# Attention: the causal mask added by VectorE in the score bank instead of by TensorE

## The chip, the cores and the metric

The kernel runs on one core of one Trainium2 chip. The time is device time in microseconds of one execution; the text compares medians of several executions. Of the core's engines four compute: TensorE (PE in the profile; its weight loads are PEld), VectorE (DVE), ScalarE (ACT) and GpSimd (POOL). SyncE (SP) issues the DMAs.

## The reference

Four layers with residual sums: causal attention, a mixture of experts, a state-space layer, the same mixture again. The change lies in the attention:

```python
x = x + attn(layernorm(x))                       # x: 2 x 1024 x 128
qk = x @ W_qk;  q, k = split(qk)                 # 16 heads of 64; k serves as the values too
scores = einsum('bhid,bhjd->bhij', q * 64**-0.5, k)
scores = where(triu(ones(n, n), k=1), -finfo.max, scores)
attn = softmax(scores, axis=-1)
out = einsum('bhij,bhjd->bhid', attn, k)  ...  @ W_out
```

## The kernel before

Attention works through 16 units (`UNITS`), each one batch entry and one pair of heads; head l of a pair lies on partitions 64 l to 64 l + 63. The scores are made transposed: keys on the partitions, queries along the bank. Key tile j (128 keys) meets only query tiles from j on, and `SLOTS` packs these stretches into 9 slots of 512 columns for each head of the pair. A slot is a pair of banks. A tile with query tile = key tile is a diagonal one; there are 8 in a unit, in slots 0 (one), 1, 2 (two each), 7 (one) and 8 (two). In slots 1 and 8 the second tile stands alone, a stretch of 128 columns.

To subtract each row's maximum ahead of the exponential, the scores are made once more the other way round one unit earlier, in 10 maxima fills (`MAX_FILLS`), which VectorE reduces (`maxima`: L498 with the mask `after_query` where the fill holds a diagonal tile, L494 without). The joined maxima are turned by TensorE (`turn_max`, L600), spread by VectorE (`max_rows`, L512), and added into the scores as a last matmul of each stretch (L625). Before that matmul a stretch has three products of high and low parts (L616, L618, L620) and, on a diagonal tile, four matmuls in bfloat16 of 128 columns that add the mask (L623: `mask2` times the unit matrix `eye2`, for two halves h and two heads l).

All of these fills share a ring of three pairs of banks (`ring`, `ring_uses`). A unit uses it in the order T (turned keys of the next unit), slot 0, Q (query projection of the next unit), slot 1, maxima fill 0, slot 2, fill 1, slot 3, fill 2, slot 4, fills 3 and 4, slot 5, fill 5, slot 6, fills 6, 7 and 8, slot 7, fill 9, slot 8, K (key projection of the unit after next). `pair_free` makes TensorE wait until the reader of the fill three places before has finished: ScalarE's exponential for a slot (`exponentials`, L453), VectorE's maxima for a fill, ScalarE's and VectorE's copies for K and Q.

The order on each engine is written out in five rounds (`ROUNDS`). At the head of round r TensorE runs a burst of output matmuls of the previous unit (`outputs`, L643), in rounds 1 and 3 also the denominators (`denominators`, L656). The outputs of round 0 and of round 1 need their bank back from VectorE's rescaling (`scale_out`, L521, semaphore `out_used`). GpSimd adds up the exponentials (`add_up`, L378), ScalarE inverts the denominators (L444, L446) and copies keys and queries (L423, L424, L429, L435), VectorE makes their low parts (L485, L314). The loops that the change touches:

```python
ROUNDS = [[("S", 0)], [("S", 1), ("M", 0), ("S", 2), ("M", 1)], [("S", 3), ("M", 2), ("S", 4), ("M", 3), ("M", 4)],
          [("S", 5), ("M", 5), ("S", 6), ("M", 6), ("M", 7)], [("M", 8), ("S", 7), ("M", 9), ("S", 8)]]
```

"S" is a slot of this unit, "M" a maxima fill of the next. The last unit has no "M".

## Time and profile before

| | |
|---|---|
| median of 3 runs | 796.08 us (795.87 to 797.96) |
| profiled execution | 797.62 us |
| its span, first to last instruction | 795.8 us, granted TensorE clock 0.983 on the mean |
| attention's units | from about 42 to 496 us of the span |
| score matmuls of the mask (L623) | 512, all between 43.8 and 488.2 us |

The profile comes from one execution. Its rows name engine, line, operation and tiles by the program's names, with the tile written before the arrow. Busy time of TensorE is that of modelled ends, so that overlapping matmuls count for more than the queue spends on them; the starts of successive rows are the better measure. In a timeline a row merges several alike instructions (x2, x4); its length then runs from the start of the first to the end of the last. Idle time ahead of a row stands in brackets with what ended it.

### The profile page before, as it was taken

What the parts mean: (1) busy time and instruction counts of PE and PEld (TensorE: products, weight loads), DVE (VectorE), ACT (ScalarE), POOL (GpSimd) and SP (SyncE); (2) the same over time, 40 slices, a digit from 0 to 9 for tenths busy, and PEclk for the clock granted to TensorE, in tenths of its full rate; (3) what the DMA queues carried; (4) which work ended last, traced back from release to release, by engine and by line L of the source; (5) the groups of instructions that cost most, each with busy time, mean ns of one, the idle gap of its engine ahead of it and who ended that gap; (6) DMA issues with size and microseconds to landing.
All of it is one profiled execution on the core that took longest, in us unless ns stands there. A gap on an engine that the chain in (4) does not pass through costs nothing. (4 is left out here: it accounts for less than half of the span.)

```text
span 795.8 us, 14382 instructions
## 1 busy us (share of the span) xinstructions
PE 738.3 (93%) x5520; PEld 499.9 (63%) x5520; DVE 455.8 (57%) x1216; ACT 386.8 (49%) x476; POOL 429.4 (54%) x311
## 2 busy tenths in 40 slices
PE   2789999999999999999999998999989999689998
PEld 1456556555655655655655554887878875468887
DVE  5765665665565675565566540257565547665542
ACT  2355546545555555554654544235753543465421
POOL 3346865765675685685676568015455331345443
PEclk9699999999999999999999999999999999799999
DMA  2000000000000000000000000733233000033232
GB/s 66 7 2 1 2 8 1 7 2 1 8 2 1 8 1 1 8 2 1 1 2 1 28 1 1 174 80 100 77 93 92 17 1 0 2 109 105 92 99 80
DMA packets 29752, 25.56 MB, mean 32 GB/s; under 512 B 10162, under 2 KB 21236, under 8 KB 29684
## 3 DMA queue, kind: packets, MB, share of 16 engines
q1 hardware_dynamic: 29684, 24.64, 10.6%
q8 instruction: 44, 0.72, 0.4%
q14 instruction: 24, 0.20, 0.1%
HBM read 23.32 MB, written 1.31 MB: 31 GB/s over the span
## 5 line engine op out<-in xcount | busy, mean ns | idle before, releaser
L378 POOL TENSOR_TENSOR all_x<-all_x,at_probs 128x1024 f32<-128x1024 f32 (+3 forms) x128 | 221.9, 1733 | 35.7 <-ACT at_probs L453 21.0
L453 ACT ACTIVATE at_probs<-at_ring 128x1024 f32<-128x1024 f32 x144 | 147.2, 1023 | 114.1 <-PE at_ring L625 107.3
L498 DVE CUSTOM_DVE_ANT_0 at_ring<-at_ring,at_after_query 128x128 f32<-128x128 f32 (+3 forms) x256 | 119.5, 520 | 74.4 <-PE at_ring L590 74.4
L643 PE MATMUL at_out<-at_probs,at_k_nat 128*64 128x512 f32 (+3 forms) x768 | 140.3, 494 | 1.1 <-DVE a_attn_t L521 0.9
L1091 POOL TENSOR_TENSOR m_prod<-m_gate,m_wb 128x512 f32<-128x512 f32 x64 | 83.0, 1304 | 97.7 <-ACT m_gate L946 93.6
L378 POOL TENSOR_TENSOR all_x<-at_probs 128x768 f32<-128x768 f32 (+1 forms) x32 | 67.1, 2095 | 126.7 <-ACT at_probs L453 126.6
L643 PEld LDWEIGHTS at_out<-at_probs,at_k_nat 128*64 128x64 f32 x768 | 49.2, 136 | 69.9 <-issue 66.0
L494 DVE TENSOR_REDUCE at_half_max<-at_ring 128x2 f32<-128x1024 f32 x64 | 75.4, 1221 | 12.2 <-PE at_ring L590 12.2
L1000 DVE TENSOR_TENSOR m_hid<-m_prod,m_u 128x512 f32<-128x512 f32 x64 | 43.4, 685 | 66.4 <-POOL m_prod L1091 66.2
L616 PE MATMUL at_ring<-at_qh,at_kh 64*128 64x512 f32 (+3 forms) x384 | 73.6, 380 | 6.2 <-DVE at_m_rows L512 2.6
L866 PEld LDWEIGHTS m_acc<-rest_wd,m_hid 128*128 128x128 f32 x576 | 74.7, 191 | 5.9
L625 PE MATMUL at_ring<-at_m_rows,at_ones_r 64*128 64x512 f32 (+3 forms) x384 | 76.0, 392 | 0.0
L866 PE MATMUL m_acc<-rest_wd,m_hid 128*128 128x128 f32 x576 | 75.2, 275 | 0.0
L946 ACT ACTIVATE m_gate<-m_g 128x512 f32<-128x512 f32 x72 | 42.6, 598 | 66.3 <-PE m_g L858 65.0
L590 PE MATMUL at_ring<-at_kh,at_qh 64*128 64x512 f32 (+3 forms) x384 | 65.5, 390 | 8.5 <-DVE at_half_max L498 2.4
L616 PEld LDWEIGHTS at_ring<-at_qh,at_kh 64*128 64x128 f32 x384 | 36.5, 187 | 52.8 <-issue 37.2
L618 PE MATMUL at_ring<-at_ql,at_kh 64*128 64x512 f32 (+3 forms) x384 | 67.0, 345 | 0.0
L620 PE MATMUL at_ring<-at_qh,at_kl 64*128 64x512 f32 (+3 forms) x384 | 66.9, 344 | 0.0
L590 PEld LDWEIGHTS at_ring<-at_kh,at_qh 64*128 64x128 f32 x384 | 36.4, 190 | 29.3 <-issue 26.0
L485 DVE TENSOR_TENSOR at_ql<-at_ring,at_qh 128x1024 fp32r<-128x1024 f32 x16 | 19.6, 1225 | 55.5 <-ACT at_qh L429 55.5
L444 ACT ACTIVATE at_inv<-at_misc 128x512 f32<-128x512 f32 x32 | 19.1, 598 | 65.3 <-PE at_misc L656 65.3
L620 PEld LDWEIGHTS at_ring<-at_qh,at_kl 64*128 64x128 f32 x384 | 36.4, 186 | 4.3
(234 smaller groups left out, 1284.1 us busy)
## 6 DMA issues: line engine op xcount, KB each, us to landing
m_wb<-m_wt_far SPq DMA_DIRECT2D x128, 128.0 KB, 3.0
all_x<-in_L_attn_a_x SPq DMA_DIRECT2D x8, 256.0 KB, 3.8
at_w_raw<-in_L_attn_a_W_qk SPq DMA_DIRECT2D x8, 128.0 KB, 2.5
out<-all_x SPq DMA_DIRECT2D x4, 256.0 KB, 3.0
a_room<-in_L_attn_a_W_out SPq DMA_DIRECT2D x1, 512.0 KB, 3.9
m_raw_wg<-in_L_ffn_experts_wg SPq DMA_DIRECT2D x1, 512.0 KB, 4.6
m_raw_wu<-in_L_ffn_experts_wu SPq DMA_DIRECT2D x1, 512.0 KB, 4.2
rest_wd<-in_L_ffn_experts_wd SPq DMA_DIRECT2D x1, 512.0 KB, 4.2
```

Source lines behind the costliest of these rows:

```text
L378: return pool.tensor_tensor(sums[:, :, a * P:b * P], left, right, ALU.add)
L453: act.activation(probs[:, :, slot * BANK:(slot + 1) * BANK], pair("S", unit, slot)[:, :, :], ACT.Exp, scale=BETA).then_inc(exp_done, 1)
L494: last = dve.reduce_max(half_max[:, :, i, out], pair("M", unit, m)[:, :, at:at + w], AX.X)
L498: last = dve.tensor_tensor_reduce(out=sums_ps, in0=sums_ps, in1=after_query[:, BANK - w:BANK], scale=1.0, scalar=MASKED, op0=ALU.add, op1= ...
L590: last = pe.matmul(out[:, l, at:at + (b - a) * P], qh[u][rows(l), i * P:(i + 1) * P], kh[u][rows(l), a * P:b * P], start=True, stop=True)
L616: pe.matmul(to[l], kh[u][rows(l), keys], qh[u][rows(l), q], start=True, stop=False)
L618: pe.matmul(to[l], kh[u][rows(l), keys], ql[u][rows(l), q], start=False, stop=False)
L620: pe.matmul(to[l], kl[u][rows(l), keys], qh[u][rows(l), q], start=False, stop=False)
L625: last = pe.matmul(to[l], ones_r[rows(l), :], m_rows[u][rows(l), q], start=False, stop=True)
L643: last = pe.matmul(out_ps[rows(l), o:o + (b - a) * P], k_nat[g % 3][:, j, rows(l)], probs[:, l, at:at + (b - a) * P], start=(j == 0), stop ...
L866: last = pe.matmul(acc[:, t * P:(t + 1) * P], hid[g % BUFS][:, t * P:(t + 1) * P], f.wd[:, st, :], start=(st == 0 and t == 0), stop=(st == ...
L1091: pool.tensor_tensor(prod[g % BUFS][:, :], gate[g % BUFS][:, :], wb[q % SPREAD][:, :], ALU.mult)\
```

## The change

The bfloat16 tiles `eye2` and `mask2` and the four mask matmuls of a diagonal tile are gone from TensorE. GpSimd makes one 128 x 128 tile `late_key` instead. VectorE gets `mask_scores`: one instruction for a slot with diagonal tiles adds `late_key` to the slot's one or two diagonal tiles of both heads, in the bank. It waits for the slot's scores and signals `masked`, for which ScalarE's exponential of these slots now waits in place of `scores_ready`. On VectorE the add of slot 0 stands ahead of the rescaling in round 0, and the others at the slot's place in the round, in the order of `ROUNDS`.

```diff
--- before.py
+++ after.py
@@ -210,6 +210,7 @@
 NBURST = len(BURSTS)
 ROUNDS = [[("S", 0)], [("S", 1), ("M", 0), ("S", 2), ("M", 1)], [("S", 3), ("M", 2), ("S", 4), ("M", 3), ("M", 4)],
           [("S", 5), ("M", 5), ("S", 6), ("M", 6), ("M", 7)], [("M", 8), ("S", 7), ("M", 9), ("S", 8)]]
+DIAGONAL = [slot for slot in range(NSLOT) if any(a == j for j, a, _ in SLOTS[slot])]
 FIRST_OF_HALF = {0: 0, 1: 1}
 BURST_OF = [max(r for r, b in enumerate(BURSTS) if any(s == slot for s, _ in b)) for slot in range(NSLOT)]
 
@@ -257,7 +258,7 @@
         neg_pick = s.sb("neg_pick", [P, QT])
         ones_r = s.sb("ones_r", [P, P], F32R)
         ones = s.sb("ones", [P, DH])
-        eye2, mask2 = s.sb("eye2", [P, 2, P], BF16), s.sb("mask2", [P, 2, P], BF16)
+        late_key = s.sb("late_key", [P, P])
         after_query = s.sb("after_query", [P, BANK])
 
         ring = [s.stack.enter_context(nc.psum_tensor(f"at_ring{i}", [P, 2, BANK], FP32)) for i in range(3)]
@@ -268,6 +269,7 @@
         proj_ready, hi_done, kt_done = s.sem("proj_ready"), s.sem("hi_done"), s.sem("kt_done")
         k_low, q_low = s.sem("k_low"), s.sem("q_low")
         knat_ps_ready, knat_done = s.sem("knat_ps_ready"), s.sem("knat_done")
+        masked = s.sem("masked")
         max_ready, max_taken, row_max_done = s.sem("max_ready"), s.sem("max_taken"), s.sem("row_max_done")
         rows_ps_ready, rows_done = s.sem("rows_ps_ready"), s.sem("rows_done")
         scores_ready, exp_done, av_done, summed = s.sem("scores_ready"), s.sem("exp_done"), s.sem("av_done"), s.sem("summed_up")
@@ -327,19 +329,16 @@
 
         def set_up(pool):
             split_w(pool, 0)
-            pool.memset(eye2[:, :, :], 0.0).then_inc(consts, 1)
-            pool.memset(mask2[:, :, :], 0.0).then_inc(consts, 1)
+            pool.memset(late_key[:, :], 0.0).then_inc(consts, 1)
             pool.memset(neg_pick[:, :], 0.0).then_inc(consts, 1)
             pool.memset(after_query[:, :], 0.0).then_inc(consts, 1)
-            pool.wait_ge(consts, 4)
+            pool.wait_ge(consts, 3)
             pool.affine_select(out=after_query[:, BANK - P:BANK], in_=after_query[:, BANK - P:BANK], compare_op=ALU.is_ge,
                                fill=MASKED, base=0, pattern=[[-1, P]], channel_multiplier=1).then_inc(consts, 1)
+            pool.affine_select(out=late_key[:, :], in_=late_key[:, :], compare_op=ALU.is_ge, fill=MASKED,
+                               base=0, pattern=[[1, P]], channel_multiplier=-1).then_inc(consts, 1)
             pool.wait_ge(consts, 5)
             for l in range(2):
-                pool.affine_select(out=eye2[rows(l), :, :], in_=eye2[rows(l), :, :], compare_op=ALU.not_equal, fill=1.0,
...
-                pool.affine_select(out=mask2[rows(l), :, :], in_=mask2[rows(l), :, :], compare_op=ALU.is_ge, fill=MASKED,
...
                 pool.affine_select(out=neg_pick[rows(l), :], in_=neg_pick[rows(l), :], compare_op=ALU.not_equal, fill=-1.0,
                                    base=0, pattern=[[-1, QT]], channel_multiplier=1).then_inc(consts, 1)
 
@@ -446,7 +445,10 @@
                     act.activation(inv[half][:, :], inv[half][:, :], ACT.Exp, scale=-1.0).then_inc(inv_done, 1)
 
                 def exponentials(unit, slot):
-                    act.wait_ge(scores_ready, 2 * (NSLOT * unit + slot) + 2)
+                    if slot in DIAGONAL:
+                        act.wait_ge(masked, len(DIAGONAL) * unit + DIAGONAL.index(slot) + 1)
+                    else:
+                        act.wait_ge(scores_ready, 2 * (NSLOT * unit + slot) + 2)
                     if unit:
                         act.wait_ge(av_done, 2 * (NBURST * (unit - 1) + BURST_OF[slot]) + 2)
                         act.wait_ge(summed, NSUM * (unit - 1) + SUMMED_AT[slot] + 1)
@@ -506,6 +508,15 @@
                     wait(dve, rows_ps_ready, 2 * unit)
                     dve.reduce_max(row_max[:, :, 0:QT], half_max[:, :, :, :], AX.X).then_inc(row_max_done, 1)
 
+                def mask_scores(unit, slot):
+
+                    dve.wait_ge(scores_ready, 2 * (NSLOT * unit + slot) + 2)
+                    at = [(at_slot(slot, seg) - slot * BANK) // P for seg, (j, a, _) in enumerate(SLOTS[slot]) if a == j]
+                    tiles = pair("S", unit, slot)[:, :, :].rearrange("p l (s c) -> p l s c", c=P)
+                    own = tiles[:, :, 0:at[-1] + 1:max(at[-1], 1), :]
+                    dve.tensor_tensor(own, own, late_key[:, :].unsqueeze(1).unsqueeze(1).to_broadcast([P, 2, len(at), P]),
+                                      ALU.add).then_inc(masked, 1)
+
                 def max_rows(unit):
 
                     dve.wait_ge(rows_ps_ready, 2 * unit + 2)
@@ -535,11 +546,14 @@
                         if r == 0:
                             if unit == 0:
                                 max_rows(0)
+                            mask_scores(unit, 0)
                             if unit:
                                 scale_out(unit - 1, 0)
                             if more:
                                 queries_low(unit + 1)
                         for what, m in row:
+                            if what == "S" and m in DIAGONAL and r:
+                                mask_scores(unit, m)
                             if what == "M" and more:
                                 maxima(unit + 1, m)
                         if r == NBURST - 1:
@@ -618,9 +632,6 @@
                             pe.matmul(to[l], kh[u][rows(l), keys], ql[u][rows(l), q], start=False, stop=False)
                         for l in range(2):
                             pe.matmul(to[l], kl[u][rows(l), keys], qh[u][rows(l), q], start=False, stop=False)
-                        for h in range(2 if a == j else 0):
-                            for l in range(2):
-                                pe.matmul(to[l][:, 0:P], mask2[rows(l), h, :], eye2[rows(l), h, :], start=False, stop=False)
                         for l in range(2):
                             last = pe.matmul(to[l], ones_r[rows(l), :], m_rows[u][rows(l), q], start=False, stop=True)
                             if seg + 1 == len(SLOTS[slot]):
...
```

(The waits for `consts` of VectorE and TensorE ahead of the first maxima go from 11 to 7.)

TensorE, round 1, slot 1 of a unit, before: the three products and the mask of its first stretch (384 columns), the row maximum, and the second stretch of 128 columns.

```order
L620 MATMUL at_ring<-at_qh,at_kl 128x384 x2
L623 MATMUL at_ring<-at_eye,at_mask 128x128 x4
L625 MATMUL at_ring<-at_m_rows,at_ones_r 128x384 x2
L616 MATMUL at_ring<-at_qh,at_kh 128x128 x2
L618 MATMUL at_ring<-at_ql,at_kh 128x128 x2
L620 MATMUL at_ring<-at_qh,at_kl 128x128 x2
L623 MATMUL at_ring<-at_eye,at_mask 128x128 x4
L625 MATMUL at_ring<-at_m_rows,at_ones_r 128x128 x2
```

The same place after the change, up to the first maxima fill (L604 was L590, L636 was L625):

```order
L634 MATMUL at_ring<-at_qh,at_kl 128x384 x2
L636 MATMUL at_ring<-at_m_rows,at_ones_r 128x384 x2
L630 MATMUL at_ring<-at_qh,at_kh 128x128 x2
L632 MATMUL at_ring<-at_ql,at_kh 128x128 x2
L634 MATMUL at_ring<-at_qh,at_kl 128x128 x2
L636 MATMUL at_ring<-at_m_rows,at_ones_r 128x128 x2
L604 MATMUL at_ring<-at_kh,at_qh 128x128 [waits at_exp_done,at_hi_done]
```

Only the mask matmuls have left; the waits of TensorE are the same. VectorE, from the end of round 4 over round 0 into round 1 of the next unit, before:

```order
L507 TENSOR_REDUCE at_row_max<-at_half_max 128x2x8 [waits at_rows_ps_ready,at_max_taken]
L521 TENSOR_TENSOR a_attn_t<-at_out,at_inv 128x512 [waits at_av_done,at_inv_done]
L512 TENSOR_TENSOR at_m_rows<-at_misc,at_neg_pick 128x1024 [waits at_rows_ps_ready]
L314 TENSOR_TENSOR at_kl<-a_room,at_kh 128x1024 [waits at_hi_done]
L521 TENSOR_TENSOR a_attn_t<-at_out,at_inv 128x512 [waits at_av_done,at_inv_done]
L485 TENSOR_TENSOR at_ql<-at_ring,at_qh 128x1024 [waits at_hi_done]
L498 ISA at_ring,at_half_max<-at_ring,at_after_query 128x128 [waits at_max_ready]
```

The same stretch after the change (L509 was L507, L532 was L521, L523 was L512, L316 was L314, L487 was L485, L500 was L498):

```order
L517 TENSOR_TENSOR at_ring<-at_ring,at_late_key 128x2x2x128 [waits at_scores_ready]
L509 TENSOR_REDUCE at_row_max<-at_half_max 128x2x8 [waits at_rows_ps_ready,at_max_taken]
L532 TENSOR_TENSOR a_attn_t<-at_out,at_inv 128x512 [waits at_av_done,at_inv_done]
L523 TENSOR_TENSOR at_m_rows<-at_misc,at_neg_pick 128x1024 [waits at_rows_ps_ready]
L316 TENSOR_TENSOR at_kl<-a_room,at_kh 128x1024 [waits at_hi_done]
L517 TENSOR_TENSOR at_ring<-at_ring,at_late_key 128x2x128 [waits at_scores_ready]
L532 TENSOR_TENSOR a_attn_t<-at_out,at_inv 128x512 [waits at_av_done,at_inv_done]
L487 TENSOR_TENSOR at_ql<-at_ring,at_qh 128x1024 [waits at_hi_done]
L517 TENSOR_TENSOR at_ring<-at_ring,at_late_key 128x2x2x128 [waits at_scores_ready]
L500 ISA at_ring,at_half_max<-at_ring,at_after_query 128x128 [waits at_max_ready]
```

The adds of slot 8, slot 0 and slot 1 (L517) have come in: ahead of the joined maxima, ahead of the second rescaling, and ahead of the maxima of fill 0.

## Rows read from the trace of the kernel before

**Rows 1.** Busy time, share of the span and instructions of each engine, from the page.

```profile
PE 738.3 (93%) x5520; PEld 499.9 (63%) x5520; DVE 455.8 (57%) x1216; ACT 386.8 (49%) x476; POOL 429.4 (54%) x311
```

**Rows 2.** Windows, 28 us of attention: length, busy us (instructions), clock, DMA share, GB/s.

```profile
154.00:182.00 28.00, 27.55 (x236) 16.18 (x234) 17.17 (x42) 15.23 (x18) 19.11 (x13) 1.00 0.02 6
```

**Rows 3.** Waits, 40 to 510 us: who waited for whom, us, times, longest.

```profile
PEld at_ring L616 <- DVE at_half_max L498: 9.5, 16, 1.0
...
PE at_ring L590 <- ACT at_probs L453: 1.3, 7, 0.3
```

**Rows 4.** Timeline of TensorE, first output matmuls of two successive units (start us, us).

```profile
151.85 2.32 PE L643 MATMUL at_out<-at_probs,at_k_nat 128*64 128x512 f32 x16
...
180.62 2.32 PE L643 MATMUL at_out<-at_probs,at_k_nat 128*64 128x512 f32 x16
```

**Rows 5.** Groups by line and form, 40 to 510 us: busy us, mean ns, idle before.

```profile
L498 DVE CUSTOM_DVE_ANT_0 at_ring<-at_ring,at_after_query 128x512 f32<-128x512 f32 x60 | 40.5, 716 | 2.9 <-PE at_ring L590 2.9
...
L623 PE MATMUL at_ring<-at_eye,at_mask 64*128 64x128 bf16 x512 | 37.0, 223 | 0.0
...
L498 DVE CUSTOM_DVE_ANT_0 at_ring<-at_ring,at_after_query 128x256 f32<-128x256 f32 x60 | 25.5, 466 | 0.0
...
L485 DVE TENSOR_TENSOR at_ql<-at_ring,at_qh 128x1024 fp32r<-128x1024 f32 x15 | 18.4, 1225 | 48.9 <-ACT at_qh L429 48.9
```

**Rows 6.** Timeline, round 1 of a unit: TensorE and slot 1's exponential.

```profile
160.26 0.34 PE L620 MATMUL at_ring<-at_qh,at_kl 64*128 64x384 f32 x2
160.43 0.29 PE L623 MATMUL at_ring<-at_eye,at_mask 64*128 64x128 bf16 x4
160.53 0.42 PE L625 MATMUL at_ring<-at_m_rows,at_ones_r 64*128 64x384 f32 x2
...
160.78 0.22 PE L616 MATMUL at_ring<-at_qh,at_kh 64*128 64x128 f32 x2
...
160.95 0.28 PE L620 MATMUL at_ring<-at_qh,at_kl 64*128 64x128 f32 x2
161.07 0.29 PE L623 MATMUL at_ring<-at_eye,at_mask 64*128 64x128 bf16 x4
161.17 0.31 PE L625 MATMUL at_ring<-at_m_rows,at_ones_r 64*128 64x128 f32 x2
...
161.31 0.45 PE L590 MATMUL at_ring<-at_kh,at_qh 64*128 64x128 f32 x4
...
161.54 1.02 ACT L453 ACTIVATE at_probs<-at_ring 128x1024 f32<-128x1024 f32 x1 [0.34 <-PE at_ring L625]
...
162.90 0.39 PE L590 MATMUL at_ring<-at_kh,at_qh 64*128 64x512 f32 x2
```

**Rows 7.** Timeline, round 4: end of fill 8's maxima, slot 8, rescaling, key projection.

```profile
176.95 0.14 DVE L498 DVE_READ_ACCUMULATOR2_ANT at_half_max<- 128x1 f32 x1
...
177.14 0.44 PE L616 MATMUL at_ring<-at_qh,at_kh 64*128 64x384 f32 x2
...
177.42 0.34 PE L618 MATMUL at_ring<-at_ql,at_kh 64*128 64x384 f32 x2
...
178.62 0.68 DVE L521 TENSOR_TENSOR a_attn_t<-at_out,at_inv 128x512 f32<-128x512 f32 x1
178.75 0.50 PE L567 MATMUL at_ring<-all_xhi,at_w_hi 128*128 128x512 f32 x1
```

**Rows 8.** Timeline, round 3: exponentials of slots 5 and 6, and maxima fill 6.

```profile
171.43 2.08 ACT L453 ACTIVATE at_probs<-at_ring 128x1024 f32<-128x1024 f32 x2
...
172.58 0.77 PE L590 MATMUL at_ring<-at_kh,at_qh 64*128 64x512 f32 x4 [0.17 <-ACT at_probs L453]
```

**Rows 9.** Timeline of ScalarE, round 0: the copy of the next queries.

```profile
157.61 1.02 ACT L429 ACTIVATE at_qh<-at_ring 128x1024 fp32r<-128x1024 f32 x1 [0.54 <-PE at_ring L569]
```

**Rows 10.** Timeline of GpSimd, the last unit's sums.

```profile
475.90 1.82 POOL L378 TENSOR_TENSOR all_x<-at_probs 128x768 f32<-128x768 f32 x1 [5.02 <-ACT at_probs L453]
...
483.25 11.64 POOL L378 TENSOR_TENSOR all_x<-all_x,at_probs 128x512 f32<-128x512 f32 x6
```

More of the change, by code:

```diff
@@ L329, in set_up @@
             split_w(pool, 0)
-            pool.memset(eye2[:, :, :], 0.0).then_inc(consts, 1)
-            pool.memset(mask2[:, :, :], 0.0).then_inc(consts, 1)
+            pool.memset(late_key[:, :], 0.0).then_inc(consts, 1)
             pool.memset(neg_pick[:, :], 0.0).then_inc(consts, 1)
             pool.memset(after_query[:, :], 0.0).then_inc(consts, 1)
-            pool.wait_ge(consts, 4)
+            pool.wait_ge(consts, 3)
             pool.affine_select(out=after_query[:, BANK - P:BANK], in_=after_query[:, BANK - P:BANK], compare_op=ALU.is_ge,
                                fill=MASKED, base=0, pattern=[[-1, P]], channel_multiplier=1).then_inc(consts, 1)
+            pool.affine_select(out=late_key[:, :], in_=late_key[:, :], compare_op=ALU.is_ge, fill=MASKED,
+                               base=0, pattern=[[1, P]], channel_multiplier=-1).then_inc(consts, 1)
             pool.wait_ge(consts, 5)
             for l in range(2):
-                pool.affine_select(out=eye2[rows(l), :, :], in_=eye2[rows(l), :, :], compare_op=ALU.not_equal, fill=1.0,
-                                   base=0, pattern=[[DH, 2], [-1, P]], channel_multiplier=1).then_inc(consts, 1)
-                pool.affine_select(out=mask2[rows(l), :, :], in_=mask2[rows(l), :, :], compare_op=ALU.is_ge, fill=MASKED,
-                                   base=0, pattern=[[DH, 2], [-1, P]], channel_multiplier=1).then_inc(consts, 1)
                 pool.affine_select(out=neg_pick[rows(l), :], in_=neg_pick[rows(l), :], compare_op=ALU.not_equal, fill=-1.0,
@@ L524, in _ @@
                 queries_low(0)
-                dve.wait_ge(consts, 11)
+                dve.wait_ge(consts, 7)
                 for m in range(NMAX):
@@ L661, in _ @@
                 turn_keys(0)
-                pe.wait_ge(consts, 11)
+                pe.wait_ge(consts, 7)
                 pe.wait_ge(cleared, 4)
```

## Prediction

> **What bounds the kernel now.** I read the busy shares first [rows 1]: TensorE is busy 93% of the span, and no other engine over 57%. The windows say where: in one unit's length of attention TensorE is busy 27.55 of 28 us at a granted clock of 1.00, VectorE 17.17, ScalarE 15.23 and GpSimd 19.11 [rows 2]. Matmul ends are modelled, so I then took the waits and the times from start to start. The whole attention holds few waits of TensorE [rows 3]: 16 before a score fill for VectorE's maxima (9.5 us on the weight load), 7 before a maxima fill for ScalarE's exponentials (1.3 us). So TensorE's queue sets the pace nearly everywhere, one unit takes 28.8 us (its first output matmuls start at 151.85, the next unit's at 180.62 [rows 4]), and what matters is whether a ring pair is handed back in time. The ring has three pairs: each fill waits for the reader of the fill three before it.
>
> **What is removed.** 512 mask matmuls [rows 5], 4 for each of 8 diagonal tiles in 16 units. Their mean of 223 ns is no price, since they overlap. By start times the four of a tile take 0.10 us (160.43 to 160.53, and 161.07 to 161.17 [rows 6]). The row-maximum matmul behind them is also slower: with 384 columns it takes 0.25 us to the next start (160.53 to 160.78), where the same width without masks ahead takes 0.17 (160.26 to 160.43); with 128 columns 0.14 (161.17 to 161.31) against 0.12 (160.95 to 161.07). I take 0.175 us a wide tile and 0.13 a 128-column one. A unit has 6 wide tiles and 2 narrow ones (the seconds of slots 1 and 8): 6 x 0.175 + 2 x 0.13 = 1.31 us, and 16 units 21.0 us of TensorE's queue.
>
> **What is added.** In each unit VectorE adds the mask in 5 instructions, two of one tile (2 x 128 columns, slots 0 and 7) and three of two tiles (512 elements, slots 1, 2 and 8). No row adds in the bank from a broadcast; the nearest are the masked maxima, which read and write the bank: 716 ns at 512 elements and 466 at 256, and the plain multiply of 512 took 0.68 [rows 5, 7]. I take 0.70 and 0.45 us. Bounds for 0.70: below 0.466, the row of half as many elements; above 1.225, the row of twice as many. VectorE gets 16 x (3 x 0.70 + 2 x 0.45) = 48 us more; at 17.17 of 28 it has the room. What costs is not the load but the place: for these five slots ScalarE's exponential waits for the add, and the pair is free later. A handover takes 0.06 us from TensorE (161.17 + 0.31, then 161.54 [rows 6]), 0.05 from VectorE (176.95 + 0.14, then 177.14 [rows 7]), 0.13 from ScalarE to TensorE (the first of two exponentials at 171.43 ends 172.45, and maxima fill 6 starts 172.58 [rows 8]).
>
> **Round 0.** Slot 0's fill is 0.175 us shorter. Its add (0.45 + 0.05) makes the exponential later by 0.50 - 0.175 = 0.33 us. Behind it on ScalarE stands the copy of the next queries, which had 0.54 us of idle time ahead of it [rows 9] and is itself wanted 0.175 sooner: 0.37 is left, so it still runs in time. The rescaling of the previous unit now stands behind this add on VectorE; it takes 0.68, and a whole query projection of TensorE lies between the end of slot 0 and the output matmuls that want its bank. Gain 0.175.
>
> **Round 1, the place that decides.** Slots 1 and 2 need 0.305 and 0.35 less. But maxima fill 1 takes the pair of slot 1. Today slot 1 is full at 161.48, its exponential runs 161.54 to 162.56, and the fill starts at 162.90 without waiting. After the change slot 1 is full at 161.18; add 161.24 to 161.94; exponential 161.99 to 163.01; fill at 163.14, where TensorE would be there at 162.90 - 0.655 = 162.25. So it waits 0.9 us and starts 0.24 later than today. A pair that starts after a wait also shows its weight load: slot 8 after its wait takes 0.28 to the next start (177.14 to 177.42 [rows 7]) against 0.17 for the same width, so 0.09 more. Loss 0.33, and the 0.655 is gone. Slot 2's add stands behind fill 0's maxima on VectorE (four, the longer two of 466 ns), and its exponential ends about 2 us behind slot 1's; its pair is wanted by maxima fill 2, which comes a burst of output matmuls and a full score fill after fill 1, so that is in time. On VectorE fill 1's maxima move with the fill. Rounds 2 and 3 have no diagonal tiles and only shift.
>
> **Round 4.** Slot 8 starts at 177.14 today, waiting for the maxima of fill 8 (end 177.09 [rows 7]), and that stays; slot 7's 0.175 goes into this wait. Slot 8 is 0.305 shorter, so the key projection behind it could start at 178.45 instead of 178.75. It takes the pair of slot 7. Slot 7's add stands behind fill 8's maxima: 177.03 to 177.48, exponential 177.53 to 178.55, projection at 178.68. Gain 0.07. The next things late are on VectorE: slot 8's add stands ahead of the rescaling, which ran 178.62 to 179.30 [rows 7]. With both adds ahead of it, 0.40 and 0.65 us net of overlaps, its end comes to about 180.3. TensorE's output matmuls, which need its bank, start at 180.62 - 0.07 = 180.55 [rows 4]: a margin of 0.2 to 0.3. Slot 8's exponential ends at about 180.55, and the key copies behind it start some 0.1 later than today, beside other work.
>
> **The sum.** A unit: -0.175 + 0.33 - 0.07 = +0.085 us; 15 units +1.3. The last unit has no maxima, and its end hangs on GpSimd, which adds probabilities without a break from the first exponentials on (475.90) to 494.89, when the denominators can start [rows 10]. Its start moves with slot 1's exponential: +0.45 later, less 0.175: +0.27. The set-up on GpSimd loses some small instructions that nobody waits for: 0. In the first unit the masks run at the lower clock level; I count that as 0 too. Together +1.5 us. The profiled execution took 797.62 us, its span 795.8, so 799.1 for it; against the median of 796.08, which it exceeds by 1.5, I forecast **797.6**.
>
> **A rule weighed.** The row shows TensorE busy 27.55 of 28 us, but its weight loads only 16.18, below VectorE's 17.17 and GpSimd's 19.11 [rows 2]. The Trainium skill (Perfetto Trace Analysis, Identifying the Most-Contended Engine) says to relieve the most contended engine first, and to judge TensorE by the share of its weight loads, not of its matmuls. By the matmul share the rule gives the full gain; by its own gauge the change moves work onto an engine as loaded as TensorE, and gives none.
>
> **The rivals.**
> - *TensorE's saving comes through* (7%): 796.1 - 21.0 = 775. For it: TensorE's share. Against: the pair of slot 1 would have to be free at 162.25, before its exponential could end even without an add. By the trace that is nearly excluded.
> - *A part gets through* (14%): the pair restarts without the 0.09, and the key projection is not held: -0.175 + 0.24 - 0.305 = -0.24 a unit, 792.7 with the last unit. Decides if slot 7's add ends by 177.2.
> - *The masks are worth less* (13%): the slower row-maximum matmul behind them isn't their doing, only the 0.10 goes. Then -0.10 in round 0, slot 1 is full 0.10 later (+0.43), and round 4 gains 0.07: +0.26 a unit, 800.3.
> - *The add is dear* (14%), the rival on the slow side: at 0.95 us for two tiles and 0.57 for one, midway to the upper bound, round 1 loses 0.25 more and round 4 0.12 more, so +0.455 a unit: 803. From 0.76 us on, the result is slower by over 0.3%. At the bound itself (1.225 and 0.68) slot 8's add and slot 7's eat that margin before the output matmuls too, about +0.9 a unit: 811.
> - *The change doesn't move the work*: excluded, since the order of the changed program has the adds and no mask matmuls.
>
> **How the numbers follow.** The forecast case has 52%, with about 1.5 us either way from handovers of 0.05 us in 15 units, so 796 to 799. A measurement of this kernel tells 0.3% (2.4 us) from no change: 793.7 to 798.5. The forecast case lies in it with some 38 points and above it with 13; part-gain lies below with 10 points, in it with 4; full gain is below; of the two slow rivals 3 points stay within. That gives faster 0.18, same 0.45, slower 0.37. The range 792.5 to 802.5 leaves out the full gain, the dearer half of the dear adds and the far side of the part-gain, 2 in 10.
>
> **What would show it.** TensorE has 512 matmuls less; VectorE has 80 adds of about 0.70 and 0.45 us and 48 us more busy time. The wait of the maxima fills for the exponentials, 1.3 us today, grows to over 10 us, at fill 1 in every unit; key projections wait for slot 7's exponential some 0.2 us. The unit's length stays 28.8 to 28.9 us. I am wrong if the unit is under 28.6 us (fill 1 doesn't wait, or the adds are short) or over 29.1 (adds above 0.8 us, or output matmuls waiting for the rescaling).

## The result and the profile after

| | before | after |
|---|---|---|
| median of 9 runs each | 796.60 us (795.87 to 797.96) | 798.76 us (798.08 to 801.62) |
| profiled execution | 797.62 us | 801.62 us |
| its span, granted clock | 795.8 us, 0.983 | 799.8 us, 0.979 |
| length of a steady unit (median of 13 of the 16) | 28.77 us | 28.74 us |

The ratio of the runs is 1.0035, 95% interval 1.0022 to 1.0047; the two medians alone lie 2.2 us or 0.27% apart. So the kernel is a little slower, and the 0.3% from which the prediction calls a result slower lies inside the interval. 512 matmuls left TensorE, and nothing was gained by it. The busy line of the page of the changed kernel, beside [rows 1]:

```profile
PE 724.1 (91%) x5008; PEld 492.6 (62%) x5008; DVE 497.2 (62%) x1296; ACT 385.9 (48%) x476; POOL 423.5 (53%) x307
```

TensorE has 14.2 us less (19.1 less in a second execution, in which its clock did not fall as described below), VectorE 41.4 us more. The same 28 us window as [rows 2] (length, busy us and instructions of PE, PEld, DVE, ACT, POOL, clock, DMA share, GB/s) no longer has TensorE full:

```profile
154.00:182.00 28.00, 26.64 (x208) 15.55 (x206) 19.56 (x46) 15.40 (x18) 18.94 (x13) 1.00 0.02 6
```

Waits of the changed kernel, 40 to 515 us, as in [rows 3] (us, times, longest), and the two forms of the add from its groups by form:

```profile
ACT at_probs L455 <- DVE at_ring L517: 82.5, 71, 3.9
...
PE at_ring L604 <- ACT at_probs L455: 14.2, 32, 0.8
...
PEld at_ring L630 <- DVE at_half_max L500: 11.7, 15, 1.0
```

```profile
L517 DVE TENSOR_TENSOR at_ring<-at_ring,at_late_key 128x512 f32<-128x512 f32 x48 | 34.5, 719 | 24.4 <-PE at_ring L636 24.4
...
L517 DVE TENSOR_TENSOR at_ring<-at_ring,at_late_key 128x256 f32<-128x256 f32 x32 | 14.3, 448 | 23.5 <-PE at_ring L636 23.5
```

The maxima fills' wait for the exponentials went from 1.3 to 14.2 us, in 32 places, with 0.7 to 0.8 us at fill 1 of a unit. The wait ahead of slot 8 [rows 3] grew from 9.5 to 11.7 us: slot 7's 0.175 us went into it. The place that decides, in a steady unit of the changed kernel:

```profile
163.17 0.44 PE L630 MATMUL at_ring<-at_qh,at_kh 64*128 64x384 f32 x2
...
164.26 0.28 PE L636 MATMUL at_ring<-at_m_rows,at_ones_r 64*128 64x128 f32 x2
...
164.37 0.44 PE L604 MATMUL at_ring<-at_kh,at_qh 64*128 64x128 f32 x4
...
164.60 0.70 DVE L517 TENSOR_TENSOR at_ring<-at_ring,at_late_key 128x512 f32<-128x512 f32 x1 [1.34 <-PE at_ring L636]
...
165.34 1.02 ACT L455 ACTIVATE at_probs<-at_ring 128x1024 f32<-128x1024 f32 x1 [0.76 <-DVE at_ring L517]
...
166.50 0.50 PE L604 MATMUL at_ring<-at_kh,at_qh 64*128 64x512 f32 x2 [0.74 <-ACT at_probs L455]
...
166.93 1.08 PE L654 MATMUL at_out<-at_probs,at_k_nat 128*64 128x512 f32 x4
```

Slot 1 starts at 163.17 and the fill behind it (fill 0) at 164.37: 1.20 us, where before has slot 1 at 159.80 (rows below) and fill 0 at 161.31 [rows 6], 1.51. So the masks' 0.31 us came off. But fill 1 waits for the add and the exponential, and the output matmuls start 3.76 us behind slot 1 instead of 3.42. From the same view of before:

```profile
154.62 0.47 PE L616 MATMUL at_ring<-at_qh,at_kh 64*128 64x512 f32 x2
...
155.91 0.50 PE L567 MATMUL at_ring<-all_xhi,at_w_hi 128*128 128x512 f32 x1
...
157.50 1.51 PE L643 MATMUL at_out<-at_probs,at_k_nat 128*64 128x512 f32 x8
...
159.80 0.44 PE L616 MATMUL at_ring<-at_qh,at_kh 64*128 64x384 f32 x2
...
162.24 0.28 PE L616 MATMUL at_ring<-at_qh,at_kh 64*128 64x256 f32 x2
...
163.22 1.08 PE L643 MATMUL at_out<-at_probs,at_k_nat 128*64 128x512 f32 x4
```

Rounds 4 and 0 of the changed kernel, which lie just ahead of the slot 1 shown above:

```profile
151.88 0.47 DVE L517 TENSOR_TENSOR at_ring<-at_ring,at_late_key 128x256 f32<-128x256 f32 x1
...
152.07 0.44 PE L630 MATMUL at_ring<-at_qh,at_kh 64*128 64x384 f32 x2 [0.32 <-DVE at_half_max L500]
...
153.55 0.48 PE L581 MATMUL at_ring<-all_xhi,at_w_hi 128*128 128x512 f32 x1
...
154.23 0.68 DVE L532 TENSOR_TENSOR a_attn_t<-at_out,at_inv 128x512 f32<-128x512 f32 x1
...
155.39 2.32 PE L654 MATMUL at_out<-at_probs,at_k_nat 128*64 128x512 f32 x16
...
158.17 0.48 PE L630 MATMUL at_ring<-at_qh,at_kh 64*128 64x512 f32 x2
...
159.28 0.50 PE L581 MATMUL at_ring<-all_xhi,at_w_hi 128*128 128x512 f32 x1
```

Slot 0 to the query projection takes 1.11 us instead of 1.29 (154.62 to 155.91), slot 8 to the key projection 1.48 instead of 1.61 [rows 7]. A steady unit is then -0.18 + 0.34 - 0.13, and -0.05 over the remaining pieces: -0.02 us by these starts, against -0.03 by the lengths of the units (28.74 less 28.77). The 13 units together take 373.68 to 374.13 us in two executions of the changed kernel, against 374.06 before.

So what the change costs comes from the ends of the attention. I divided the span where VectorE spreads the joined maxima of each unit (`max_rows`), up to the last denominators. The second execution of the changed kernel is that of the last experiment:

| us | before | after | after, again |
|---|---|---|---|
| start of the second unit | 65.77 | 68.93 | 66.28 |
| 13 steady units | 374.06 | 374.13 | 373.68 |
| the one from the 15th to the last | 27.18 | 27.99 | 28.02 |
| the last, to its denominators | 27.93 | 29.35 | 29.38 |
| the layers behind | 300.9 | 299.4 | 299.5 |

The last two of the attention lose 0.8 and 1.4 us in both executions. The layers behind are not touched by the change; over the fourteen kept profiles they take 299.4 to 301.2 us, so the spans of two single executions can differ by up to 1.8 us for reasons outside the attention. The start of the second unit differs by 2.65 us between the two executions of the changed kernel: 0.77 us are there already when the first unit begins (40.78 against 40.01 us), 1.88 come within it (28.15 against 26.27 us), and the unit behind it is longer by 0.47 (29.21 against 28.74). The clock windows go with that (before, then after, then after again):

```profile
65.00:70.00 5.00, 5.00 (x52) 2.90 (x51) 3.81 (x3) 3.30 (x5) 4.63 (x3) 1.00 0.00 0
```

```profile
60.00:65.00 5.00, 4.06 (x30) 3.06 (x29) 4.55 (x15) 1.02 (x1) 4.68 (x3) 0.78 0.01 3
65.00:70.00 5.00, 5.00 (x18) 2.94 (x18) 1.85 (x3) 2.75 (x3) 4.30 (x3) 0.54 0.00 0
```

```profile
65.00:70.00 5.00, 5.00 (x49) 2.90 (x47) 2.95 (x2) 3.77 (x5) 4.71 (x3) 1.00 0.00 0
```

In the profiled execution the granted clock had reached 1.00 at 50 us and fell back to 0.78 and 0.54, that is, TensorE was granted 1.2 instead of 2.4 GHz for about 6.8 of these 10 us. The trace has 18 matmuls in 65 to 70 us, where those of the other two have 52 and 49.

### The profile page after: what moved, and what is told of

The parts are those of the page before. It is cut to its first block and busy times, and to the rows that moved or that the text cites. A ratio compares the mean times of both kernels' runs of the same rounds, so it can differ in the third digit from the quotient of the medians.

```text
span 799.8 us, 13431 instructions
## 1 busy us (share of the span) xinstructions
PE 724.1 (91%) x5008; PEld 492.6 (62%) x5008; DVE 497.2 (62%) x1296; ACT 385.9 (48%) x476; POOL 423.5 (53%) x307
## 3 DMA queue, kind: packets, MB, share of 16 engines
HBM read 23.32 MB, written 1.31 MB: 31 GB/s over the span
## 5 line engine op out<-in xcount | busy, mean ns | idle before, releaser
L377 POOL TENSOR_TENSOR all_x<-all_x,at_probs 128x1024 f32<-128x1024 f32 (+3 forms) x128 | 218.3, 1706 | 44.8 <-ACT at_probs L455 30.7
L500 DVE CUSTOM_DVE_ANT_0 at_ring<-at_ring,at_after_query 128x128 f32<-128x128 f32 (+3 forms) x256 | 119.1, 519 | 45.4 <-PE at_ring L604 45.4
L604 PE MATMUL at_ring<-at_kh,at_qh 64*128 64x512 f32 (+3 forms) x384 | 67.3, 397 | 20.2 <-ACT at_probs L455 14.2
L517 DVE TENSOR_TENSOR at_ring<-at_ring,at_late_key 128x512 f32<-128x512 f32 (+1 forms) x80 | 48.9, 611 | 47.9 <-PE at_ring L636 47.9
L636 PE MATMUL at_ring<-at_m_rows,at_ones_r 64*128 64x512 f32 (+3 forms) x384 | 67.2, 344 | 0.0
L604 PEld LDWEIGHTS at_ring<-at_kh,at_qh 64*128 64x128 f32 x384 | 36.7, 189 | 44.6 <-issue 40.8
L487 DVE TENSOR_TENSOR at_ql<-at_ring,at_qh 128x1024 fp32r<-128x1024 f32 x16 | 19.6, 1225 | 32.1 <-ACT at_qh L428 32.1
```

Source lines behind the costliest of these rows:

```text
L377: return pool.tensor_tensor(sums[:, :, a * P:b * P], left, right, ALU.add)
L500: last = dve.tensor_tensor_reduce(out=sums_ps, in0=sums_ps, in1=after_query[:, BANK - w:BANK], scale=1.0, scalar=MASKED, op0=ALU.add, op1= ...
L604: last = pe.matmul(out[:, l, at:at + (b - a) * P], qh[u][rows(l), i * P:(i + 1) * P], kh[u][rows(l), a * P:b * P], start=True, stop=True)
L636: last = pe.matmul(to[l], ones_r[rows(l), :], m_rows[u][rows(l), q], start=False, stop=True)
```

## The experiments

All times are medians; the time of before beside each is from the same chip. Line numbers shift a little from kernel to kernel.

**1. The whole mask taken away.** Neither engine adds the mask to the scores; that is left out of the computation (the maxima keep theirs).

```diff
-                            mask_scores(unit, 0)
...
-                            if what == "S" and m in DIAGONAL and r:
-                                mask_scores(unit, m)
...
-                    if slot in DIAGONAL:
-                        act.wait_ge(masked, len(DIAGONAL) * unit + DIAGONAL.index(slot) + 1)
```

> The changed kernel with the adds left out and nothing in their place: no mask is applied anywhere, the exponential waits for the scores as before. It gives what the mask's leaving TensorE is worth when nothing is put in its place. Theory of the ring (a fill waits for the reader three places before): the unit is 0.90 us shorter than the 28.77 of before (slot 0 0.18, round 1 only 0.42 of its 0.66 because maxima fill 1 then waits for slot 1's exponential, round 4 0.30, slot 7's share vanishing in the wait for the maxima of fill 8), 27.87 us, and the time about 782.5. Rival, TensorE's queue alone counts: 1.31 us a unit, 27.46, and 775.6. Rival, the price of a mask matmul is only the 0.10 us of its own starts: 0.8 us a unit at most, 785 or more.

Measured: 784.21 us against 797.05, ratio 0.9833 (0.9818 to 0.9848), steady unit 27.90 us. Without any mask a unit loses 0.87 us, not the 1.31 that the matmuls occupy: the rest disappears in waits that are there without any mask. It is a measure of what there was to win from the masks in this order of work, some 13 us.

**2. and 3. The change by halves.** In 2 the masks of slots 1 and 2 stay on TensorE, in 3 only these two go to VectorE (`DIAGONAL = [1, 2]`).

```diff
-DIAGONAL = [slot for slot in range(NSLOT) if any(a == j for j, a, _ in SLOTS[slot])]
+DIAGONAL = [0, 7, 8]
...
+                        for h in range(2 if a == j and slot not in DIAGONAL else 0):
+                            for l in range(2):
+                                pe.matmul(to[l][:, 0:P], mask2[rows(l), h, :], eye2[rows(l), h, :], start=False, stop=False)
```

> The change for slots 0, 7 and 8 only; slots 1 and 2 keep their mask matmuls on TensorE and their exponentials wait for the scores. Theory of the ring, with the loss in round 1: the unit is 28.45 us (28.77 less 0.18 in round 0, 0.13 at the key projection and 0.03), and less the losses of the last two units (0.8 and 1.1 us, where slot 8's add stands before the joined maxima and slot 0's before the rescaling with no projection to cover them) the time is about 794.0, 2.6 below the kernel before. Rival, the loss comes from slots 0, 7 and 8 (adds ahead of the rescaling and the joined maxima): the unit stays at 28.74 or grows.

Measured: 793.16 against 797.05, 0.9955 (0.9942 to 0.9969), unit 28.42.

> The other part alone: slots 1 and 2 masked by VectorE, slots 0, 7 and 8 by TensorE as before. Theory of the ring: the unit is 28.77 + 0.34 = 29.1 us, the time 802, 5.5 above before; maxima fill 1 waits some 0.75 us for the exponential in each unit, and no wait of the output matmuls for the rescaling is added. Rival (slots 1 and 2 are neutral): 28.8 us, 797.

Measured: 802.37, 1.0068 (1.0054 to 1.0082), unit 29.10. The halves are -0.35 and +0.33 us a unit, and their sum of -0.02 is, to 0.01, what the whole change gives (28.74 against 28.77). Round 1 alone makes the kernel slower, rounds 0 and 4 alone make it faster. The wait of the maxima fills for the exponentials goes with slots 1 and 2 (2, then 3):

```profile
PE at_ring L612 <- ACT at_probs L462: 1.8, 10, 0.3
```

```profile
PE at_ring L612 <- ACT at_probs L462: 14.0, 31, 0.8
```

**4. VectorE's order mended at the end.** In the last unit the rescaling goes ahead of slot 0's add; in the one before it, the joined maxima go ahead of slot 8's add.

```diff
+                            if not more:
+                                scale_out(unit - 1, 0)
                             mask_scores(unit, 0)
-                            if unit:
+                            if unit and more:
                                 scale_out(unit - 1, 0)
...
+                            if what == "S" and m == NSLOT - 1 and unit + 2 == UNITS:
+                                join_maxima(unit + 1)
```

> The changed kernel with the order on VectorE mended at its two ends: in the last unit the rescaling stands ahead of slot 0's add, and in the last unit but one the joined maxima ahead of slot 8's add. Theory that the loss against before (+2.2 us in the medians) sits at these ends: the steady unit stays 28.74, the last unit but one is 0.8 us shorter, the last one 1.1, and the time is about 796.9, the same as before. Rival, the loss is spread over the units: under 0.3 us gained. The fall of TensorE's clock in the first unit, seen in the profiled execution, should come or stay away as in the changed kernel, since nothing there is touched.

Measured: 800.57 against 797.05, 1.0042 (1.0028 to 1.0056). This missed; the median did not move. In the profile the last unit is as expected: 28.17 instead of 29.35 us. The changed kernel has there, and then the mended one:

```profile
474.75 0.43 DVE L517 TENSOR_TENSOR at_ring<-at_ring,at_late_key 128x256 f32<-128x256 f32 x1 [2.48 <-PE at_ring L636]
475.09 0.68 DVE L532 TENSOR_TENSOR a_attn_t<-at_out,at_inv 128x512 f32<-128x512 f32 x1
...
475.83 1.51 PE L654 MATMUL at_out<-at_probs,at_k_nat 128*64 128x512 f32 x8 [1.14 <-DVE a_attn_t L532]
```

```profile
470.97 0.69 DVE L532 TENSOR_TENSOR a_attn_t<-at_out,at_inv 128x512 f32<-128x512 f32 x1 [1.46 <-PE at_out L658]
...
471.91 1.51 PE L658 MATMUL at_out<-at_probs,at_k_nat 128*64 128x512 f32 x8
472.05 0.43 DVE L517 TENSOR_TENSOR at_ring<-at_ring,at_late_key 128x256 f32<-128x256 f32 x1 [0.39 <-PE at_ring L640]
```

The last unit has no query projection, so the output matmuls of round 1 come straight behind slot 0, and with the add ahead of the rescaling they wait 1.14 us. The unit before it gained nothing (28.10). It has no key projection, so `turn_max` comes straight behind slot 8 and waits for the joined maxima; in the changed kernel, then in the mended one:

```profile
470.54 0.44 PE L614 MATMUL at_misc<-all_ident,at_row_max 128*64 128x128 f32 x4 [0.95 <-DVE at_row_max L509]
471.18 2.38 PE L654 MATMUL at_out<-at_probs,at_k_nat 128*64 128x512 f32 x16 [0.20 <-issue]
```

```profile
467.24 0.44 PE L618 MATMUL at_misc<-all_ident,at_row_max 128*64 128x128 f32 x4 [0.48 <-DVE at_row_max L509]
...
467.70 0.68 DVE L532 TENSOR_TENSOR a_attn_t<-at_out,at_inv 128x512 f32<-128x512 f32 x1
...
468.48 2.37 PE L658 MATMUL at_out<-at_probs,at_k_nat 128*64 128x512 f32 x16 [0.80 <-issue]
```

The turn's wait halved, but the rescaling now stood behind the add (467.70 to 468.38), and the output matmuls started 0.10 us behind its end: the wait went one instruction down the queue. (The profile puts this wait down to `issue`; that it is the rescaling is read from the program's order and the 0.10 us.) Why the median does not show the 1.2 us of the last unit stays open. Three of the five runs had a mean clock of 0.979 to 0.981 and took 800.57 to 801.01 us, but the other two, at 0.985, took 799.05 and 800.04 and show no gain either beside the changed kernel.

**5. One add twice.** Slot 1's add is done a second time, with zeros.

```diff
+                    if times == 2:
+                        dve.tensor_tensor(own, own, no_mask[:, :].unsqueeze(1).unsqueeze(1).to_broadcast([P, 2, len(at), P]),
+                                          ALU.add).then_inc(halfway, 1)
+                        dve.wait_ge(halfway, unit + 1)
```

> The changed kernel with a second instruction on slot 1 in every unit: ahead of the mask, VectorE adds a tile of zeros to the same two tiles, and the mask's add waits for it, so that slot 1's exponential comes one add of 0.70 us and a handover later. Theory of the ring (the add of slot 1 lies whole on the path add, exponential, maxima fill 1): maxima fill 1 waits 0.75 to 0.8 us longer, the unit is 29.5 us, the time about 811, 12.5 above the changed kernel. Rival (VectorE has room at 60% busy, an add more is hidden): under 1 us in all.

Measured: 810.78 against 796.06, 1.0184 (1.0167 to 1.0201), unit 29.47 (the median of the 13; two of them took 30.6 in the profiled execution, which was the slowest of the four): +0.73 us, the whole length of one add. Nothing covers what is added to the chain behind slot 1, and the fills' wait for the exponentials grows by 11 us in 15 units:

```profile
PE at_ring L610 <- ACT at_probs L456: 25.2, 31, 1.5
```

**6. and 8. Other work under the wait.** TensorE's denominators of the previous unit (four matmuls with nothing pressing behind them) move from the head of round 1 to just ahead of maxima fill 1, and ScalarE inverts them behind slot 4's exponential. In 6 this is done to the changed kernel, in 8, as a control, to the kernel before.

```diff
-                        if r == 1 and unit:
+                        if r == 1 and unit == UNITS:
                             denominators(unit - 1, 1)
...
                             if what == "S":
                                 scores(unit, n)
+                                if n == 2 and unit:
+                                    denominators(unit - 1, 1)
```

> The changed kernel with other work of TensorE put into the gap: the denominators of the previous unit (0.95 us of TensorE) move from ahead of slot 1 to behind slot 2, right ahead of maxima fill 1, and their inversion on ScalarE moves behind slot 4's exponential. Nothing else changes. Theory of the ring: slot 1 is full 0.95 us earlier, its exponential is done when fill 1's turn comes, the wait of 0.75 us and the slow restart go, and the unit falls from 28.74 to 27.8 us; the time is about 784. Rival (ScalarE or VectorE bind as soon as that wait is gone, at fill 2, 3 or in round 4): 28.2 us or more a unit, 790 or more. Rival (the loss has nothing to do with fill 1): 28.74, no gain.

Measured: 789.0 against 796.06, 0.9908 (0.9891 to 0.9924), unit 28.07 instead of 28.74.

> Control: the kernel before, masks on TensorE, with the same move of the denominators and their inversion. Nothing waits at maxima fill 1 in it, so by the theory of the ring the move alone gives nothing: 28.77 us a unit and 797 (0.2 either way). Rival (the move itself is what helps, with or without the masks on VectorE): the time falls by several us.

Measured: 800.36 against 796.06, 1.0054 (1.0037 to 1.0071), unit 29.10. The move is worth 0.67 us a unit in the changed kernel and costs 0.33 in the one before. So the wait was there to be filled, and the move has a price of its own, which I had set at nothing; with it both 6 and 8 missed their expected units, 27.8 and 28.77. Its rows, in 6 and then in 8:

```profile
162.54 1.08 PE L667 MATMUL at_misc<-all_x,at_ones 128*64 128x512 f32 x4
163.55 0.49 PE L604 MATMUL at_ring<-at_kh,at_qh 64*128 64x512 f32 x2
163.97 1.08 PE L654 MATMUL at_out<-at_probs,at_k_nat 128*64 128x512 f32 x4
```

```profile
158.91 1.51 PE L643 MATMUL at_out<-at_probs,at_k_nat 128*64 128x512 f32 x8
160.35 0.44 PE L616 MATMUL at_ring<-at_qh,at_kh 64*128 64x384 f32 x2
...
162.81 0.28 PE L616 MATMUL at_ring<-at_qh,at_kh 64*128 64x256 f32 x2
...
163.55 1.08 PE L656 MATMUL at_misc<-all_x,at_ones 128*64 128x512 f32 x4
164.56 0.50 PE L590 MATMUL at_ring<-at_kh,at_qh 64*128 64x512 f32 x2
164.99 1.08 PE L643 MATMUL at_out<-at_probs,at_k_nat 128*64 128x512 f32 x4
```

In 6 fill 1 follows the denominators with no wait, and yet takes 0.42 us to the next start. In 8 the four denominators take 1.01 us between the score matmuls and fill 1, but leaving them out behind the output matmuls shortened that stretch only from 2.30 to 1.44 us, 0.86. Fill 1 takes 0.43 to the next start instead of 0.32 [rows 6], and slot 2's last stretch 0.74 to the next start instead of 0.66 (162.24 to 162.90 in the kernel before). 0.15 + 0.11 + 0.08 = 0.34, the measured 0.33. In the changed kernel fill 1 already took 0.43 us, behind its wait, so there the move costs only some 0.24: of the 0.90 us by which fill 1 was held (165.60, a stretch's 0.12 behind 165.48, to 166.50) 0.67 come through. Both forms have four matmuls of 512 columns; what differs is how often matmuls of 64 rows (scores, maxima) and of 128 rows by 64 columns (outputs, denominators) follow one another: two more such changes in a unit. That these changes are the cause is read from the rows; no experiment tells it from another reason.

**7. The best of these.** 6, with slot 7's mask back on TensorE and the end mended as in 4.

```diff
-DIAGONAL = [slot for slot in range(NSLOT) if any(a == j for j, a, _ in SLOTS[slot])]
+DIAGONAL = [0, 1, 2, 8]
```

> The previous kernel with slot 7's mask back on TensorE, where its 0.18 us vanish in the wait of slot 8's fill for the maxima of fill 8, so that the key projection no longer waits for slot 7's exponential; and with the order on VectorE mended in the last two units. Theory of the ring: the key projection starts 0.2 us earlier, 27.6 us a unit, some 1 us less at the end: about 780. Rival (the output matmuls then wait for the rescaling behind slot 8's add instead): 27.8 us as without it, 783.

Measured: **784.90** against 796.06, 0.9863 (0.9847 to 0.9879), unit 27.91: 1.4% faster than the kernel before. TensorE waits for fill 8's maxima ahead of slot 8 in any case, so slot 7's mask costs nothing there, while its add had stood in the way of fill 9's maxima and of the key projection. The unit is 0.31 us above the expected 27.6, which stood on the 27.8 expected of experiment 6, itself missed by 0.27 because the price of the move was left out. The unit's 0.16 us on experiment 6 belong to slot 7's mask, since the mended end does not touch a steady unit.

**9. to 12. The two ends, told apart.** 9 is the changed kernel with the first unit's masks on TensorE; 10 is that with the end mended as in 4; 11 is 7 with the first unit on TensorE; 12 is the changed kernel again, beside them on the same chip.

```diff
-                    if slot in DIAGONAL:
-                        act.wait_ge(masked, len(DIAGONAL) * unit + DIAGONAL.index(slot) + 1)
+                    if unit and slot in DIAGONAL:
+                        act.wait_ge(masked, len(DIAGONAL) * (unit - 1) + DIAGONAL.index(slot) + 1)
...
+                        for h in range(2 if a == j and (unit == 0 or slot not in DIAGONAL) else 0):
```

> The changed kernel, but in the first of the 16 units the masks stay on TensorE. The first unit has no output matmuls, so TensorE is early at every fill, and VectorE and ScalarE set its length. Theory: the adds lengthen it in full (26.3 us against 24.7 in the kernel before, and 28.2 where TensorE's clock fell again after the pauses); with TensorE's masks it is back at 24.7 to 25.0, no fall of the clock between 60 and 70 us, and the median is 1.3 to 2 us below the changed kernel's, about 797.2. Rival (the first unit's length is chance from the clock's start and not from the adds): no difference beyond 0.5 us.

> The previous kernel, and in the last unit the rescaling ahead of slot 0's add (with the joined maxima first in the last unit but one). Theory: 1.0 us less than the previous kernel at the end of attention, about 796.2, level with the kernel before, because with both ends mended only the steady units' 28.74 against 28.77 are left. Rival (the ends don't matter): the same as the previous kernel.

> The best kernel so far (denominators moved, slot 7 on TensorE, ends mended: 784.9) with the first unit's masks on TensorE: by the same theory 0.7 to 1.5 us less, about 783.8. Steady unit unchanged at 27.91.

> The changed kernel itself, beside the others on this chip. 798.8; steady unit 28.74. Where its profile shows no fall of TensorE's clock within the first unit, that unit should be 26.3 us long; where it shows one, 28.

| | us | ratio to before, 796.55 us |
|---|---|---|
| 12, the changed kernel | 800.15 (7 runs) | 1.0043 (1.0028 to 1.0059) |
| 9, first unit on TensorE | 798.43 (11 runs) | 1.0021 (1.0011 to 1.0030) |
| 10, and the end mended | 797.73 (11 runs) | 1.0012 (1.0003 to 1.0021) |
| 11, best version, first unit on TensorE | 785.24 (4 runs) | 0.9853 (0.9836 to 0.9870) |

The two ends together are worth 2.4 us of the 3.6 that 12 lies above before. The intervals of 12 and 10 lie apart, so that much is shown (what is left in 10, 1.2 us, is what its profile has for the last two units, 28.11 - 27.18 and 28.17 - 27.93); those of 12 and 9, and of 9 and 10, overlap, so its split into 1.7 for the first unit and 0.7 for the last ones is not. Of the 16 runs of the changed kernel (after and 12), five had a granted clock of 0.979 to 0.981 over the span and took 801.46 to 801.78 us; the other eleven, at 0.985 to 0.987, took 798.0 to 800.15, with a median of 798.72, only 0.3 above 9. So most of the 1.7 comes from the five slower runs, and how many of them fall among the runs moves the median of the changed kernel (798.76 with two of nine, 800.15 with three of seven). Of the 26 runs of 9, 10 and 11, none had a mean clock below 0.983.

The mean clock is only a hint of a fall in the first unit: of the 23 runs of before beside them, six had 0.981 or 0.982 and were not slower for it (795.67 to 797.49 us), and the profile of experiment 1 has 0.980 with no fall there. The profiles themselves show the fall in two of the eight executions whose first unit has all or some of the adds (after, and experiment 6 with 0.76 and 0.56 between 60 and 70 us), and in none of the six that have none. For the best version the first unit made no difference (784.90 and 785.24), and the 783.8 expected of 11 was missed.

## Why the prediction was right, and where its sums were off

The forecast and its range held: 797.6 for a median of 796.08, +1.5 us; +2.2 us measured. On the outcome it was at the edge: it held the same (0.45) likelier than slower (0.37), with the line at 0.3%, and the ratio of 1.0035 lies just above that line, the medians' 0.27% just below. By the steps:

- **What is removed.** 1.31 us a unit of TensorE's queue: 0.31 us came off slot 1 (0.305 forecast) and 0.18 off round 0 (0.175). The rival that the masks are worth less falls. Experiment 1 shows that even without a replacement only 0.87 of it reaches the unit's length.
- **What is added.** 719 and 448 ns for forecast 700 and 450, so the dear add falls too. VectorE's busy time rose by 41.4 us rather than 48, though the adds alone are 48.8, since rows overlap: the add at 151.88 ends at 152.35, and the next row starts at 152.25.
- **Round 1.** Fill 1 starts 3.33 us behind slot 1's start (forecast 163.14 for 159.80, 3.34) and takes 0.43 us to the next start, 0.11 more than before (0.09 forecast). Loss 0.34, forecast 0.33. Experiments 3 and 5 confirm the chain: the wait goes with the adds of slots 1 and 2, and grows one for one with slot 1's.
- **Round 4.** Gain 0.13 instead of 0.07, of the 0.305 by which slot 8 is shorter; the key projection is held for the rest, as forecast. Slot 7's add starts at 151.88, with the last accumulator read of fill 8's maxima and not near its end: 0.19 us ahead of slot 8, where I had it 0.11 ahead. The margin before the output matmuls is 0.48 us (154.91 to 155.39), not 0.2 to 0.3, and nothing waits there. With 0.05 from the other pieces, the unit is -0.02 instead of +0.085, 1.6 us less over 15 units.
- **The sum.** Terms taken too low at the ends stand against this. The last unit was set at +0.27 and measured +1.4, and the one before it, which I counted as a steady one, +0.8. In round 0 I had named the cover of the rescaling, "a whole query projection of TensorE", and in round 4 the key projection is what lies between slot 8 and the turned maxima; the last units have neither. With the rescaling put back ahead (experiment 4) the last unit is 28.17, +0.24, what the sum had for it. The first unit was set at 0. It has no output matmuls between its fills, so that two fills of its rounds 1 and 2 wait for exponentials behind adds, where before had no wait (second execution of the changed kernel, below). It takes 26.3 us there and 24.7 before, but I can't give all of that to the adds: in the profiled executions of 9 and 10, whose first units are the same, it took 26.1 and 25.0. The clock at its start goes with that: from 45 to 50 us it was 0.65 in 9 and 0.88 in 10. Where it started alike (0.50, then 0.81 to 0.88 in these 5 us), the unit took 26.3 with all adds (12 and experiment 4) and 24.8 to 25.0 with none (8 and 10), which puts the adds at 1.2 to 1.5 us; the medians of 9 and of the eleven faster runs of the changed kernel show only 0.3 of it, so its size stays open. On top comes the second fall of the clock, which the profile has at some 2.3 us (1.88 in the first unit and 0.47 in the next); the five runs that may have had it were some 3 us slower than the others.

```profile
50.34 0.50 PE L604 MATMUL at_ring<-at_kh,at_qh 64*128 64x512 f32 x2 [0.54 <-ACT at_probs L455]
...
52.20 0.44 PE L604 MATMUL at_ring<-at_kh,at_qh 64*128 64x384 f32 x2 [0.43 <-ACT at_probs L455]
```

- **The cancelling.** The errors of the steady units and of the ends have opposite signs. The forecast was right in the mechanism that decides, and right in the total partly by that cancelling.
- **A rule weighed.** The Trainium skill (Perfetto Trace Analysis, Identifying the Most-Contended Engine) would have judged TensorE by its weight loads and given the change no gain; the result agrees. Experiment 7 does not bear the reason out: with VectorE still adding four of five masks, those masks off TensorE bring 1.4% once the wait at fill 1 is covered. What stood in the way was one wait in the ring, not VectorE's load.
- **The rivals.** That the saving comes through needed the pair of slot 1 free in time; TensorE stood 0.74 us idle for it. The part-gain's place and price (round 1 without its weight load, round 4 without a hold) did not occur, though the unit ended at -0.02, between it and the forecast.

## What to carry to other kernels

A matmul group taken off a full TensorE is worth its time only up to the next place where TensorE waits for a buffer; follow the buffer through its new reader chain (fill, add, exponential, fill) and compare its end with the time at which TensorE would arrive. When the chain is late, look for work in TensorE's queue with nothing pressing behind it and put it under the wait: here that turned +0.35% into -0.9%, and -1.4% with slot 7's mask given back and the end mended. Price the move too: the order of the matmuls was not free. Work out the first and last iterations on their own, since the cover that a term of the steady state names is often just what they leave out.

## What the runs showed of the hardware

- Moving four matmuls of 512 columns within TensorE's queue cost 0.33 us a unit by itself (experiment 8), 0.08 to 0.15 at each of three places where matmuls of 64-row and of 128-row tiles now follow one another or no longer stand beside their like. I had taken an order of matmuls to be free. The Trainium skill (TensorEngine Tiling (Array Packing), Key Properties) says that a change of tiling mode drains TensorE. The rows fit that, with 0.08 to 0.15 us a place, but show no drain as such, and no run tells it from weight loads that are no longer covered.
- A row-maximum matmul behind four bfloat16 masks is slower than the same without them, and that is the masks' doing: with them gone, slot 0 to the projection is 0.18 us shorter, not 0.10.
- VectorE's add in the bank with a broadcast operand costs 719 ns at 512 elements and 448 at 256, like the masked maxima beside it (710 and 467 ns).
- TensorE's granted clock reached 1.00 at 50 us and fell again to 0.78 and 0.54 between 60 and 70 us in the profiled execution of the changed kernel. TensorE had been busy 3.61 of 5 us from 50 to 55 us, against 4.81 before. The second execution was busy 3.55 of 5 us there and its clock stayed at 1.00, so the pauses of this unit do not decide it alone. None of the six profiled executions without adds in the first unit shows the fall, two of the eight with adds do; six against eight is too few to call the adds the cause. What decides it in a run is open.
